# Swapping the operands of a one-hot product and pausing GpSimd's gathers of one more tile in a DLRM/CIN kernel

## The chip, the cores and the metric

The kernel runs on one NeuronCore of a Trainium2 chip. The time is device microseconds of one execution, the median of several runs; lower is better. TensorE (PE) multiplies matrices, with its weight loads counted apart as PEld; VectorE (DVE), ScalarE (ACT) and GpSimd (POOL) work on SBUF, and SyncE (SP), ACT and POOL issue DMAs.

## The reference, cut to what matters

A batch of 1,024 rows looks up 24 embedding tables of width 16. The embeddings go through a three-layer compressed interaction network (each layer multiplies the embeddings with the layer before, field by field, and mixes with weights), whose sums over the width go with a dense context through a small MLP.

```python
e = jnp.stack([tbl_0[ids[:, 0]], tbl_1[ids[:, 1]], ..., tbl_23[ids[:, 23]]], axis=1)   # (1024, 24, 16)
# _cin_forward(X0=e, Ws=(W0, W1, W2)), 64 outputs per layer
for W in Ws:
    H_prev = Xk.shape[1]
    Wr = W.reshape(F_, H_prev, W.shape[1])
    Xk = jnp.einsum('bfd,bhd,fho->bod', X0, Xk, Wr)
    outs.append(Xk.sum(axis=2))
z = jnp.concatenate(outs, axis=1)
h = jnp.concatenate([z, dense_ctx], axis=1)
h = jnp.maximum(h @ W_top1 + b_top1, 0.0)
h = jnp.maximum(h @ W_top2 + b_top2, 0.0)
y = h @ W_top3
```

Eight of the tables have 125,000 or 12,500 rows, sixteen have 1,000 or 1,250.

## The kernel before

All is float32. The batch is cut into 8 tiles of 128 rows, and each tile into two units of 64 rows, so there are 16 units. A tile's embeddings are brought into `x0_rows` (128 rows by 24 fields by 16), stored to DRAM in `x0_dram` (the profile's x_scratch), and loaded again from there in broadcast forms: `A` (three buffers of 128x1024 a unit) and `C` (two loads a unit, and a third buffer that ScalarE copies together, `copy_c`). VectorE multiplies A by C for the first layer (L373, three products a unit) and A by `ps_b`, a spread form of the first layer's output, for the second (L383, twelve a unit); each product Z is taken up by TensorE matmuls into `ps_x`. Z has a ring of five buffers. `ps_b` is made by TensorE (`make_b`) or, from unit 4 on, partly loaded (`B_sb`) and copied into PSUM by ScalarE.

**How tile 0 gets its embeddings.** Its eight large tables are gathered by GpSimd: one indirect DMA a table (L215), 8 in all, without a pause. Its sixteen small tables are looked up with one-hot matrices, in two sets of eight tables. A set's table rows are cut into chunks of 128 (8 chunks for set 0, 10 for set 1). For each chunk VectorE compares the ids with the chunk's row numbers (L346), which gives a 128x1024 matrix of ones and zeros in a buffer Z: 128 table rows by 8 tables by 128 batch rows. TensorE then runs 8 matmuls a chunk (L406, called at L612): the table chunk (128x16) is the operand that is loaded into the array, and the ones (128x128) stream. Results of the tables lie in four column groups of 32 of the array and accumulate in `ps_b[k]`. They come out turned (width by batch row), so ScalarE copies them to `x0_small` (L838, 4 copies a set), TensorE turns them (`turn_small`, L418, 2 transposes a set), and ScalarE copies the result to `x0_rows` (L842) and stores it (L206, on ACT's queue). 18 chunks of 8 matmuls are 144 matmuls; each float32 matmul shows as two LDWEIGHTS and two MATMUL records, so 288 pairs.

**What follows.** SP waits in order for the three parts of tile 0 and loads A and C of units 0 and 1. TensorE runs 40 transposes on the identity (`keep_warm`, L412) and the three first products; then the loop over units begins.

**How tiles 1 to 7 get theirs.** GpSimd gathers all 24 tables a tile, one indirect DMA each. Tile 1's gathers follow tile 0's at once. From tile 2 on, a gather is preceded by a pause: a memset of `pause_sb` (128x288, L227) and a wait for it. Tile 2's first also waits until tile 0 is stored. SP stores a tile when its 24 gathers have landed (`store_tile`, L206) and later waits for that store before it loads C and A of the tile's first unit. SP is in order: the loads of quarters, A, C and B of other units stand in the same queue.

```python
            for f in range(FR):
                gather(0, f, first_gathered)
            for t in range(1, TILES):
                if t >= 2:
                    wait_stored(pool, t - 2)
                for f in range(F):
                    if t >= 2:
                        pool.memset(pause_sb[:, :], 0.0).then_inc(paused, 1)
                        pool.wait_ge(paused, F * (t - 2) + f + 1)
```

Of the kernel before, what the change touches and what calls it, by code (L numbers as in the profile page):

```python
# [10 lines left out]
BATCH, F, D, H, DENSE = 1024, 24, 16, 64, 16  # L11
M1, M2 = 512, 256
TILE_ROWS = 128
# [11 lines left out]
FR, HR = 8, 16  # L25
# [7 lines left out]
ZR = 5  # L33
AS = 3
WARM = (40, 16, 16, 4)
SETS = 2
# [31 lines left out]
def cin_tower(nc, dense_t, ids, tables, small_ids, small_tables, small_rows, chunks, w0a, w0b, w1, w2, wt1, bt1, wt2, bt2, wt3, ident, mask, pick, out):  # L68

    CR = small_tables.shape[0]
# [5 lines left out]
    with ctx:  # L77
        def sb(name, shape, dt=F32):
            return ctx.enter_context(nc.sbuf_tensor(name, shape, dt))
# [4 lines left out]
        def sem(name):  # L84
            return ctx.enter_context(nc.semaphore(name))

        ids_sb = sb("ids_sb", [128, TILES * F], mybir.dt.int32)
        id_sb = sb("id_sb", [128, 128])
# [3 lines left out]
        small_sb = sb("small_sb", [CR, len(HOT), FR, D])  # L92
        small_rows_sb = sb("small_rows_sb", [CR, max(chunks)])
        small_ids_sb = [sb(f"small_ids_sb{k}", [CR, FR * TILE_ROWS], mybir.dt.int32) for k in range(SETS)]
        small_ids_f32 = [sb(f"small_ids_f32_{k}", [CR, FR * TILE_ROWS]) for k in range(SETS)]

        x0_small = [sb(f"x0_small{k}", [128, 2 * TILE_ROWS]) for k in range(SETS)]
        pause_sb = sb("pause_sb", [128, PAUSE])
        w0_sb = sb("w0_sb", [128, NI, H])
        w0m_sb = sb("w0m_sb", [128, NI, H])  # L100
# [10 lines left out]
        x0_rows = [sb(f"x0_rows{p}", [128, F * D]) for p in range(2)]  # L111
# [6 lines left out]
        Z = [sb(f"Z{r}", [128, COLS]) for r in range(ZR)]  # L118
# [16 lines left out]
        ps_b = [bank(f"ps_b{e}", 2) for e in range(2)]  # L135
        ps_x2, ps_x1, ps_tower = bank("ps_x2"), bank("ps_x1"), bank("ps_tower")

        ps_turn = bank("ps_turn")
# [10 lines left out]
        ident_in, mask_in, pick_in, w0_in, w1_in, tower_in = (sem(n) for n in (  # L149
            "ident_in", "mask_in", "pick_in", "w0_in", "w1_in", "tower_in"))  # L150
# [6 lines left out]
        paused = sem("paused")  # L157

        hot_used, small_turned = sem("hot_used"), sem("small_turned")  # L160
        z_used, b_made, x2_turned, x0_turned, g_summed = (sem(n) for n in (
            "z_used", "b_made", "x2_turned", "x0_turned", "g_summed"))
        z3_summed, h1_summed, h2_summed, y_summed = (sem(n) for n in (
            "z3_summed", "h1_summed", "h2_summed", "y_summed"))

        small_copied, small_ready = sem("small_copied"), sem("small_ready")
        c_copied, b_copied = sem("c_copied"), sem("b_copied")
        x1_copied, x2_copied, x2r_copied, diag_ready, g_copied = (sem(n) for n in (
            "x1_copied", "x2_copied", "x2r_copied", "diag_ready", "g_copied"))  # L170
# [4 lines left out]
        small_ids_ready, hot_ready = sem("small_ids_ready"), sem("hot_ready")  # L175
# [34 lines left out]
        @block.gpsimd  # L210
        def _(pool):
            pool.wait_ge(ids_in, 16)

            def gather(t, f, landed):
                pool.indirect_dma_start(  # L215
                    out=x0_rows[t % 2][:, f * D:(f + 1) * D], out_offset=None, in_=tables[f],
                    in_offset=bass.IndirectOffsetOnAxis(ap=ids_sb[:, t * F + f:t * F + f + 1], axis=0),
                ).then_inc(landed, 16)
# [4 lines that stand above are left out]
                if t >= 2:  # L223
                    wait_stored(pool, t - 2)
                for f in range(F):
                    if t >= 2:
                        pool.memset(pause_sb[:, :], 0.0).then_inc(paused, 1)  # L227
                        pool.wait_ge(paused, F * (t - 2) + f + 1)

                    after(pool, z_ready, PER_SLOT * (2 * t - 5) + 2 * PER_SLOT * f // F)  # L230
                    gather(t, f, gathered[t % 2])
# [102 lines left out]

        @block.vector
        def _(dve):
            for k in range(SETS):
                nc.vector.memset(x0_small[k][:, :], 0.0).then_inc(small_ids_ready, 1)
            dve.wait_ge(small_rows_in, 16)
            for n, (k, c) in enumerate(HOT):  # L340
                if c == 0:
                    dve.wait_ge(small_ids_in[k], 16)
                    nc.vector.tensor_copy(small_ids_f32[k][:, :], small_ids_sb[k][:, :]).then_inc(small_ids_ready, 1)
                    dve.wait_ge(small_ids_ready, SETS + k + 1)
                after(dve, hot_used, n - ZR + 1)
                nc.vector.tensor_scalar(Z[n % ZR][0:CR, :], small_ids_f32[k][:, :], small_rows_sb[:, c:c + 1],  # L346
                                        None, ALU.is_equal).then_inc(hot_ready, 1)
# [57 lines left out]
        def mm(out, lhsT, rhs, start=True, stop=True):  # L405
            return nc.tensor.matmul(out, lhsT, rhs, start=start, stop=stop)  # L406

        @block.tensor
        def _(pe):
            def keep_warm(n):  # L410
                for _ in range(n):
                    nc.tensor.transpose(ps_tower[:, 0:128], id_sb[:, :], id_sb[:, :])  # L412

            def turn_small(k):
                pe.wait_ge(ident_in, 16)
                pe.wait_ge(small_copied, 4 * (k + 1))
                for half in range(2):
                    last = nc.tensor.transpose((ps_turn, ps_x2)[k][:, TILE_ROWS * half:TILE_ROWS * (half + 1)],  # L418
                                               x0_small[k][:, TILE_ROWS * half:TILE_ROWS * (half + 1)], id_sb[:, :])
                last.then_inc(small_turned, 1)  # L420

            def cross1(u, i):
                s = made_x1(u, i) - 1
# [182 lines left out]
            for n, (k, c) in enumerate(HOT):  # L606
                if c == 0:
                    pe.wait_ge(small_in[k], 16)
                pe.wait_ge(hot_ready, n + 1)
                for f in range(FR):  # L610
                    g, half = f % 4, f // 4
                    last = mm(ps_b[k][32 * g:32 * g + D, 512 * half:512 * half + TILE_ROWS], small_sb[:, n, f, :],  # L612
                              Z[n % ZR][0:CR, TILE_ROWS * f:TILE_ROWS * (f + 1)], c == 0, c == chunks[k] - 1)
                last.then_inc(hot_used, 1)
                if c == 2 and k > 0:
                    turn_small(0)
            turn_small(SETS - 1)
            keep_warm(WARM[0])
            pe.wait_ge(w0_ready, 1)
            for i in range(NI):  # L620
# [28 lines left out]
        def _(act):  # L649
# [181 lines left out]
            act.wait_ge(mask_in, 16)  # L831

            nc.scalar.copy(first_sb[:, :], mask_sb[:, :])
            act.wait_ge(small_ids_ready, SETS)
            for k in range(SETS):
                act.wait_ge(hot_used, sum(chunks[:k + 1]))
                for g in range(4):
                    nc.scalar.copy(x0_small[k][32 * g:32 * g + D, :].rearrange("p (h b) -> p h b", h=2),  # L838
                                   ps_b[k][32 * g:32 * g + D, :].rearrange("p (h b) -> p h b", h=2)[:, :, 0:TILE_ROWS])\
                        .then_inc(small_copied, 1)  # L840
                act.wait_ge(small_turned, k + 1)
                nc.scalar.copy(x0_rows[0][:, FR * D * (k + 1):FR * D * (k + 2)].rearrange("p (f d) -> p f d", d=D),  # L842
                               (ps_turn, ps_x2)[k][:, 0:2 * TILE_ROWS].rearrange("p (f e) -> p f e", e=32)[:, :, 0:D])\
                    .then_inc(small_ready, 1)
                act.wait_ge(small_ready, k + 1)
                store_rows(act, 0, slice(FR * (k + 1), FR * (k + 2)), part_stored[k + 1])
# [90 lines left out]
```

## Time and profile before

| | |
|---|---|
| median of 3 runs | 413.58 us (409.85 to 417.03) |
| the profiled execution | 417.16 us, span from first to last instruction 415.3 us |
| mean granted TensorE clock | 0.992 of full speed |
| busy | PE 363.0 us (87%), DVE 302.4 (73%), ACT 184.6 (44%), POOL 231.3 (56%) |
| DMA | 71.07 MB, mean 171 GB/s |

The profile is one execution. Its page shows the span in 40 slices of 10.4 us; a timeline row gives start, duration, engine, line, operation, output and inputs, the count of merged instructions and, in brackets, the idle time before and what ended it. "issue" means that the engine waited for nothing that the profile shows. All times below are microseconds from the span's start. L12 is line 12 of the kernel before; behind the change the same code stands some lines higher.

### The profile page before, as it was taken

The numbers are of one execution on the slowest core, as the hardware profiler recorded it, in microseconds if no ns is written. First come the engines' busy times: TensorE is split into PE (matmuls) and PEld (weight loads), VectorE is DVE, ScalarE is ACT, GpSimd is POOL, SyncE is SP. The second block draws the span as 40 slices with busy tenths as digits, with TensorE's granted clock in tenths as the row PEclk, the third lists the DMA queues.
The fourth block names the chain that finished last, engine by engine and source line by source line (L and its number), as shares of the span: only waits on it lengthen the run. The fifth ranks groups of instructions, "written<-read, shape, count | busy, mean of one in ns | idle before, by whom it ended". The sixth has DMA issues, their size and how long they took to land.

```text
span 415.3 us, 6926 instructions
## 1 busy us (share of the span) xinstructions
PE 363.0 (87%) x2624; PEld 161.1 (39%) x2624; DVE 302.4 (73%) x299; ACT 184.6 (44%) x347; POOL 231.3 (56%) x324
## 2 busy tenths in 40 slices
PE   1531485999999999898999999999899999999997
PEld 0200372523323333344343434444343354443465
DVE  3210452599698989859798989989799999898700
ACT  1000110024362426444756566565457475745374
POOL 5777106888888888888878888888830000000000
PEclk9999998899999999999999999999999999999999
DMA  7520047969988798998799989997999899941000
GB/s 217 154 42 6 2 96 170 243 134 230 209 214 208 178 242 153 235 243 196 155 227 244 240 162 228 257 253 145 234 252 261 156 238 239 225 117 36 2 1 4
DMA packets 56884, 71.07 MB, mean 171 GB/s; under 512 B 31153, under 2 KB 36017, under 8 KB 56850
## 3 DMA queue, kind: packets, MB, share of 16 engines
q1 hardware_dynamic: 49138, 69.04, 71.7%
q0 software_dynamic: 5632, 1.45, 3.4%
q8 instruction: 21, 0.34, 0.4%
q10 hardware_dynamic: 2080, 0.13, 0.3%
q14 instruction: 13, 0.11, 0.1%
HBM read 50.15 MB, written 1.58 MB: 125 GB/s over the span
## 4 chain that ended last, share of the span: by engine, by line
PE 80%; issue 9%; DMA 4%; ACT 3%; DVE 2%; another core or an unknown queue 2%; SPq 0%; DVEq 0%; ACTq 0%
PE ps_x L406 48%; PE ps_b L406 12%; PE ps_tower L406 9%; PE ps_turn L406 6%; PE ps_turn L459 2%; DMA x_scratch<-x_rows 1%; PE ps_turn L467 1%; DMA small_ids_sb<-small_ids 1%; DVE Z L383 1%; DMA C<-x_scratch 1%; PE ps_tower L412 1%; DVE Z L373 1%; ACT x_diag L691 1%; ACT C L665 0%
## 5 line engine op out<-in xcount | busy, mean ns | idle before, releaser
L383 DVE TENSOR_TENSOR Z<-A,ps_b 128x1024 f32<-128x1024 f32 x192 | 221.8, 1213 | 18.9 <-PE ps_x L406 13.6
L215 POOL DMA_INDIRECT x_rows<-tbl,ids_sb x176 | 180.4, 1025 | 52.7 <-issue 23.9
L406 PE MATMUL ps_x<-Z,w_sb 128*64 128x512 f32 x768 | 184.9, 598 | 0.9 <-DVE Z L383 0.5
L406 PEld LDWEIGHTS ps_x<-Z,w_sb 128*64 128x64 f32 x768 | 49.4, 136 | 80.8 <-issue 58.9
L373 DVE TENSOR_TENSOR Z<-A,C 128x1024 f32<-128x1024 f32 x48 | 57.4, 1222 | 30.5 <-DMA C<-x_scratch 10.4
L227 POOL MEMSET pause_sb<- 128x288 f32 x144 | 50.7, 352 | 21.4 <-DMA x_scratch<-x_rows 21.3
L691 ACT ACTIVATE x_diag<-ps_turn,mask_sb 128x192 f32<-128x192 f32 x128 | 50.6, 605 | 12.2 <-PE ps_turn L467 11.6
L406 PE MATMUL ps_b<-Z,small_sb 128*16 128x128 f32 x288 | 21.1, 357 | 34.7 <-issue 25.2
L406 PE MATMUL ps_x<-Z,w0s_sb 128*64 128x512 f32 x192 | 46.3, 608 | 5.5 <-DVE Z L373 5.3
L704 ACT COPY G<-ps_turn 128x416 f32<-128x416 f32 x31 | 15.7, 506 | 61.4 <-PE ps_turn L406 42.8
L674 ACT COPY ps_b<-B_sb 128x1024 f32<-128x1024 f32 x36 | 37.1, 1030 | 0.0
L346 DVE TENSOR_SCALAR Z<-small_ids_f,small_rows_sb 128x1024 f32<-128x1024 f32 x18 | 12.7, 750 | 33.3 <-remote 31.5
L406 PEld LDWEIGHTS ps_turn<-x_diag,x_rows 128*64 128x64 f32 x496 | 24.8, 137 | 20.6 <-issue 19.5
L406 PE MATMUL ps_b<-x_sb,pick_sb 64*128 64x512 f32 x112 | 31.3, 639 | 0.2 <-issue 0.2
L655 ACT COPY x_sb<-ps_x 128x512 f32<-128x512 f32 x16 | 9.4, 587 | 47.4 <-PE ps_x L406 47.4
L406 PE MATMUL ps_turn<-x_diag,x_rows 128*64 128x104 f32 x496 | 27.8, 254 | 1.7 <-issue 1.6
L406 PEld LDWEIGHTS ps_b<-Z,small_sb 128*16 128x16 f32 x288 | 12.3, 119 | 42.9 <-issue 32.1
L406 PEld LDWEIGHTS ps_x<-Z,w0s_sb 128*64 128x64 f32 x192 | 13.5, 139 | 33.3 <-issue 23.2
L838 ACT COPY x_small<-ps_b 16x256 f32<-16x256 f32 x8 | 2.9, 364 | 49.3 <-PE ps_b L406 49.1
L664 ACT COPY C<-C 64x1024 f32<-64x1024 f32 x15 | 15.6, 1043 | 7.6 <-DMA C<-x_scratch 7.3
L406 PE MATMUL ps_tower<-h,wt_sb 128*64 128x256 f32 (+1 forms) x112 | 15.5, 379 | 0.4 <-ACT h L774 0.4
L665 ACT COPY C<-C 64x1024 f32<-64x1024 f32 x15 | 15.7, 1044 | 0.4
(60 smaller groups left out, 192.7 us busy)
## 6 DMA issues: line engine op xcount, KB each, us to landing
A<-x_scratch SPq DMA_DIRECT2D x48, 512.0 KB
B_sb<-x_sb SPq DMA_DIRECT2D x72, 256.0 KB
C<-x_scratch SPq DMA_DIRECT2D x32, 512.0 KB
x_rows<-tbl,ids_sb POOLq DMA_INDIRECT x176
x_quarters<-x_scratch SPq DMA_DIRECT2D x16, 96.0 KB
x_scratch<-x_rows SPq DMA_DIRECT2D x7, 192.0 KB
small_ids_sb<-small_ids SPq DMA_DIRECT2D x2, 512.0 KB, 5.2
w_sb<-w SPq DMA_DIRECT2D x2, 384.0 KB
```

What stands on the lines that cost most here:

```text
L215: pool.indirect_dma_start(out=x0_rows[t % 2][:, f * D:(f + 1) * D], out_offset=None, in_=tables[f], in_offset=bass.IndirectOffsetOnAxis(ap ...
L227: pool.memset(pause_sb[:, :], 0.0).then_inc(paused, 1)
L346: nc.vector.tensor_scalar(Z[n % ZR][0:CR, :], small_ids_f32[k][:, :], small_rows_sb[:, c:c + 1], None, ALU.is_equal).then_inc(hot_ready, 1)
L373: nc.vector.tensor_tensor(Z[s % ZR][:, :], A[u % AS][i][:, :], C[u % 2][i][:, :], ALU.mult).then_inc(z_ready, 1)
L383: nc.vector.tensor_tensor(Z[s % ZR][:, :], A[u % AS][i][:, :], ps_b[j % 2][:, :], ALU.mult)\
L406: return nc.tensor.matmul(out, lhsT, rhs, start=start, stop=stop)
L655: nc.scalar.copy(x1_sb[u % 2][:, :], ps_x1[:, :]).then_inc(x1_copied, 1)
L664: nc.scalar.copy(c[NI - 1][0:64, :], c[1][64:128, :]).then_inc(c_copied, 1)
L665: nc.scalar.copy(c[NI - 1][64:128, :], c[0][0:64, :]).then_inc(c_copied, 1)
L674: nc.scalar.copy(ps_b[(k + 1) % 2][:, :], B_sb[k][:, :]).then_inc(b_copied, 1)
L691: last = nc.scalar.activation(x0_diag[u % 2][:, :, 0:F, b].rearrange("p (h k) f -> p k h f", k=2), ps_turn[:, 0:256].rearrange("p (k f h) ...
L704: nc.scalar.copy(G[:, :, at:at + ROWS_Q].rearrange("p j (k b) -> p k j b", b=RB), bank[:, 0:KB * J3 * RB].rearrange("p (k j b) -> p k j b" ...
```

## The change

Three things. (1) In tile 0's one-hot matmuls the operands trade places: the ones (128x128) are loaded into the array and the table chunk (128x16) streams. The result comes out as batch row by width, eight tables side by side in 128 columns of `ps_b[k]`, and one accumulation group runs over all of a set's matmuls. (2) What turned the result goes: the two memsets of `x0_small`, 4 copies a set, `turn_small`, and their semaphores; one ScalarE copy a set brings `ps_b[k]` to `x0_rows`. (3) The pause stands ahead of each gather of tile 1 too.

```diff
@@ gpsimd
                 for f in range(F):
-                    if t >= 2:
-                        pool.memset(pause_sb[:, :], 0.0).then_inc(paused, 1)
-                        pool.wait_ge(paused, F * (t - 2) + f + 1)
+                    pool.memset(pause_sb[:, :], 0.0).then_inc(paused, 1)
+                    pool.wait_ge(paused, F * (t - 1) + f + 1)
 
                     after(pool, z_ready, PER_SLOT * (2 * t - 5) + 2 * PER_SLOT * f // F)
                     gather(t, f, gathered[t % 2])
@@ vector
-            for k in range(SETS):
-                nc.vector.memset(x0_small[k][:, :], 0.0).then_inc(small_ids_ready, 1)
             dve.wait_ge(small_rows_in, 16)
@@ tensor
-            def turn_small(k):
-                pe.wait_ge(ident_in, 16)
-                pe.wait_ge(small_copied, 4 * (k + 1))
-                for half in range(2):
-                    last = nc.tensor.transpose((ps_turn, ps_x2)[k][:, TILE_ROWS * half:TILE_ROWS * (half + 1)],
-                                               x0_small[k][:, TILE_ROWS * half:TILE_ROWS * (half + 1)], id_sb[:, :])
-                last.then_inc(small_turned, 1)
...
                 for f in range(FR):
-                    g, half = f % 4, f // 4
-                    last = mm(ps_b[k][32 * g:32 * g + D, 512 * half:512 * half + TILE_ROWS], small_sb[:, n, f, :],
-                              Z[n % ZR][0:CR, TILE_ROWS * f:TILE_ROWS * (f + 1)], c == 0, c == chunks[k] - 1)
+
+                    last = mm(ps_b[k][:, D * f:D * (f + 1)], Z[n % ZR][0:CR, TILE_ROWS * f:TILE_ROWS * (f + 1)],
+                              small_sb[:, n, f, :], (c, f) == (0, 0), (c, f) == (chunks[k] - 1, FR - 1))
                 last.then_inc(hot_used, 1)
-                if c == 2 and k > 0:
-                    turn_small(0)
-            turn_small(SETS - 1)
+            pe.wait_ge(ident_in, 16)
             keep_warm(WARM[0])
@@ scalar
-            act.wait_ge(small_ids_ready, SETS)
             for k in range(SETS):
                 act.wait_ge(hot_used, sum(chunks[:k + 1]))
-                for g in range(4):
-                    nc.scalar.copy(x0_small[k][32 * g:32 * g + D, :].rearrange("p (h b) -> p h b", h=2),
-                                   ps_b[k][32 * g:32 * g + D, :].rearrange("p (h b) -> p h b", h=2)[:, :, 0:TILE_ROWS])\
-                        .then_inc(small_copied, 1)
-                act.wait_ge(small_turned, k + 1)
-                nc.scalar.copy(x0_rows[0][:, FR * D * (k + 1):FR * D * (k + 2)].rearrange("p (f d) -> p f d", d=D),
-                               (ps_turn, ps_x2)[k][:, 0:2 * TILE_ROWS].rearrange("p (f e) -> p f e", e=32)[:, :, 0:D])\
+                nc.scalar.copy(x0_rows[0][:, FR * D * (k + 1):FR * D * (k + 2)], ps_b[k][:, 0:FR * D])\
                     .then_inc(small_ready, 1)
```

GpSimd's order at the start, before. L215 is a gather, L227 the pause; x_rows is `x0_rows`.

```order
L215 DMA x_rows<-tbl,ids_sb 128x16 x32
L227 MEMSET pause_sb 128x288
L215 DMA x_rows<-tbl,ids_sb 128x16
L227 MEMSET pause_sb 128x288
L215 DMA x_rows<-tbl,ids_sb 128x16
```

GpSimd's order at the start, with the change (the gather is L213, the pause L224):

```order
L213 DMA x_rows<-tbl,ids_sb 128x16 x8
L224 MEMSET pause_sb 128x288
L213 DMA x_rows<-tbl,ids_sb 128x16
L224 MEMSET pause_sb 128x288
L213 DMA x_rows<-tbl,ids_sb 128x16
```

The run of gathers without a pause shrinks from 32 to 8; 24 pauses come in.

TensorE's order from its first matmul to the first product, before; the shape behind a matmul is rows of the result by columns streamed:

```order
L406 MATMUL ps_b<-Z,small_sb 16x128 x88
L418 MATMUL ps_turn<-id_sb,x_small 128x128 x2
L406 MATMUL ps_b<-Z,small_sb 16x128 x56
L418 MATMUL ps_x<-id_sb,x_small 128x128 x2
L412 MATMUL ps_tower<-id_sb 128x128 x40
L406 MATMUL ps_x<-Z,w0s_sb 64x512 x2
```

TensorE's order in the same place, with the change:

```order
L401 MATMUL ps_b<-small_sb,Z 128x16 x144
L407 MATMUL ps_tower<-id_sb 128x128 x40
L401 MATMUL ps_x<-Z,w0s_sb 64x512 x2
```

The 144 matmuls stand in one run, and the four transposes are gone. Nothing behind them moved.

ScalarE's order from the first copy of a result of tile 0 to its second store, before:

```order
L838 COPY x_small<-ps_b 16x256 x4
L842 COPY x_rows<-ps_turn 128x128
L206 DMA x_scratch<-x_rows 128x8x16
L838 COPY x_small<-ps_b 16x256 x4
L842 COPY x_rows<-ps_x 128x128
L206 DMA x_scratch<-x_rows 128x8x16
```

ScalarE's order in the same place, with the change:

```order
L821 COPY x_rows<-ps_b 128x128
L204 DMA x_scratch<-x_rows 128x8x16
L821 COPY x_rows<-ps_b 128x128
L204 DMA x_scratch<-x_rows 128x8x16
```

One copy a set stands where five copies and a wait for TensorE stood.

## Rows read from the trace of the kernel before

**Rows 1.** The page, slices of 10.4 us: PE and DMA, busy share in tenths
```profile
PE   1531485999999999898999999999899999999997
...
DMA  7520047969988798998799989997999899941000
```

**Rows 2.** The page's groups: one-hot matmuls and VectorE's comparisons (busy, mean ns, idle before)
```profile
L406 PE MATMUL ps_b<-Z,small_sb 128*16 128x128 f32 x288 | 21.1, 357 | 34.7 <-issue 25.2 <-DVE Z L346 9.3
...
L346 DVE TENSOR_SCALAR Z<-small_ids_f,small_rows_sb 128x1024 f32<-128x1024 f32 x18 | 12.7, 750 | 33.3 <-remote 31.5
```

**Rows 3.** Timeline of PE, 8 to 60 us
```profile
9.28 4.05 PE L406 MATMUL ps_b<-Z,small_sb 128*16 128x128 f32 x59 [9.28 <-DVE Z L346]
14.15 0.62 PE L406 MATMUL ps_b<-Z,small_sb 128*16 128x128 f32 x4 [0.82 <-issue]
...
44.56 0.37 PE L406 MATMUL ps_b<-Z,small_sb 128*16 128x128 f32 x1 [1.73 <-issue]
...
48.06 4.50 PE L406 MATMUL ps_b<-Z,small_sb 128*16 128x128 f32 x80 [1.03 <-issue]
...
52.87 3.25 PE L406 MATMUL ps_b<-Z,small_sb 128*16 128x128 f32 x112
```

**Rows 4.** Timeline of GpSimd: first and last gathers of tiles 0 to 2, and tile 7's last
```profile
3.01 1.08 POOL L215 DMA_INDIRECT x_rows<-tbl,ids_sb  x1 [2.56 <-DMA ids_sb<-ids]
...
12.25 1.02 POOL L215 DMA_INDIRECT x_rows<-tbl,ids_sb  x1 [0.31 <-issue]
...
42.53 0.94 POOL L215 DMA_INDIRECT x_rows<-tbl,ids_sb  x1 [0.30 <-issue]
...
64.79 0.34 POOL L227 MEMSET pause_sb<- 128x288 f32 x1 [21.31 <-DMA x_scratch<-x_rows]
...
65.47 0.95 POOL L215 DMA_INDIRECT x_rows<-tbl,ids_sb  x1 [0.34 <-POOL pause_sb L227]
...
67.04 0.95 POOL L215 DMA_INDIRECT x_rows<-tbl,ids_sb  x1 [0.27 <-POOL pause_sb L227]
...
103.61 0.95 POOL L215 DMA_INDIRECT x_rows<-tbl,ids_sb  x1 [0.27 <-POOL pause_sb L227]
...
304.75 0.95 POOL L215 DMA_INDIRECT x_rows<-tbl,ids_sb  x1 [0.27 <-issue]
```

**Rows 5.** Timeline of PE: short matmuls elsewhere, all at full clock
```profile
58.11 4.53 PE L412 MATMUL ps_tower<-id_sb 128*128 128x128 f32 x40
...
191.86 0.88 PE L406 MATMUL ps_turn<-x_diag,x_rows 128*64 128x104 f32 x16
...
387.68 0.88 PE L406 MATMUL ps_turn<-x_diag,x_rows 128*64 128x104 f32 x16
```

**Rows 6.** Timeline, all engines: from the last one-hot matmul to unit 0's first product
```profile
56.19 1.53 ACT L838 COPY x_small<-ps_b 16x256 f32<-16x256 f32 x4 [2.94 <-PE ps_b L406]
...
58.31 0.27 ACT L842 COPY x_rows<-ps_x 128x128 f32<-128x128 f32 x1 [0.59 <-PE ps_x L418]
58.60 0.37 ACTq L206 DMA_DIRECT2D x_scratch<-x_rows  x1
...
79.29 6.88 DVE L383 TENSOR_TENSOR Z<-A,ps_b 128x1024 f32<-128x1024 f32 x6 [0.59 <-PE ps_b L406]
```

**Rows 7.** SP's waits: total us, times, longest us
```profile
SPq L206 <- DMA x_rows<-tbl,ids_sb: 20.0, 2, 14.6
```

**Rows 8.** The chain of waits: one load of C from issue to landing
```profile
64.66 4.56 DMA C<-x_scratch
```

**Rows 9.** Timeline of SP and ScalarE: stores of tiles 2 and 7, unit 14's C
```profile
112.18 0.36 SPq L206 DMA_DIRECT2D x_scratch<-x_rows  x1
...
315.97 0.76 SPq L206 DMA_DIRECT2D x_scratch<-x_rows  x1
...
325.02 1.18 SPq L263 DMA_DIRECT2D C<-x_scratch  x2
...
333.99 1.04 ACT L664 COPY C<-C 64x1024 f32<-64x1024 f32 x1
```

More of the change, by code:

```diff
@@ L95, in cin_tower @@
         small_ids_f32 = [sb(f"small_ids_f32_{k}", [CR, FR * TILE_ROWS]) for k in range(SETS)]
-        x0_small = [sb(f"x0_small{k}", [128, 2 * TILE_ROWS]) for k in range(SETS)]
         pause_sb = sb("pause_sb", [128, PAUSE])
@@ L157, in cin_tower @@
         paused = sem("paused")
-        hot_used, small_turned = sem("hot_used"), sem("small_turned")
+        hot_used = sem("hot_used")
         z_used, b_made, x2_turned, x0_turned, g_summed = (sem(n) for n in (
@@ L164, in cin_tower @@
             "z3_summed", "h1_summed", "h2_summed", "y_summed"))
-        small_copied, small_ready = sem("small_copied"), sem("small_ready")
+        small_ready = sem("small_ready")
         c_copied, b_copied = sem("c_copied"), sem("b_copied")
@@ L343, in _ @@
                     nc.vector.tensor_copy(small_ids_f32[k][:, :], small_ids_sb[k][:, :]).then_inc(small_ids_ready, 1)
-                    dve.wait_ge(small_ids_ready, SETS + k + 1)
+                    dve.wait_ge(small_ids_ready, k + 1)
                 after(dve, hot_used, n - ZR + 1)
```

## Prediction, made before the result was known

> **What bounds the kernel now.** I read the page's slices first, then its groups, then the timeline of the first 80 us engine by engine, and last SP's waits. In the slices [rows 1] PE is busy in eight or nine tenths from the ninth slice on (83 us) to nearly the end, and DMA as well from the seventh; in the third to fifth slice (21 to 52 us) neither is. The start is what is slow: the first product of unit 0 begins at 79.29 [rows 6], a fifth of the span. The groups name the place [rows 2]: the one-hot matmuls have 25.2 us of "issue" idle before them, and VectorE waits 31.5 us before its comparisons, though 18 of them at 0.75 us need 12.7 us.
>
> The timeline of PE [rows 3] shows how: 59 records in 4.05 us, then ever fewer, 4 with a gap of 0.82 us behind at 14.15, single ones with 1.7 us of gap at 44.56, and at 48.06 all at once 80 in 4.50 us (VectorE's pace) and 112 in 3.25 us. 288 - 80 - 112 = 96 records took until 48. The last 37 of them took 34 us, and they are the same instructions as the fast ones. What changed at 48.06 is on GpSimd [rows 4]: the run of 32 gathers without a pause began at 3.01 and its last was issued at 42.53. Tile 1's 24 came every (42.53 - 12.25) / 24 = 1.26 us. If something behind a gather needs a fixed time and PE's instructions wait for the same thing, that time is (48.06 - 3.01) / 32 = 1.41 us, a backlog grows by 0.15 us a gather, and its end lies 4.6 us behind the end of the last gather, as it does. I call it the stall and do not know its resource. Paused gathers come every 67.04 - 65.47 = 1.57 us, longer than 1.41, so they should build no backlog; and 144 of them (64.79 to 305.70) run beside matmuls that are not slowed: 16 short records take 0.88 us at 191.86 among gathers and 0.88 us at 387.68 without any [rows 5].
>
> **The change part by part.** The sum is made against the profiled execution, 417.16 us (span 415.3 plus 1.9), which lies 3.6 above the median of 413.58.
>
> *Pauses, on PE.* The stall goes, except what the first 8 gathers leave: 3.01 + 8 x 1.41 = 14.3, while the ninth gather would now be issued at about 12.25 + 1.02 + 0.35 + 0.27 = 13.9. That backlog of 0.4 us shrinks by 0.16 a gather and is gone near 18.5. At four records in 0.62 + 0.82 us [rows 3] from 13.3 to 18.5 PE would lose some 4 us; with a smaller backlog I take 2.5, bounds 0 and 4.
>
> *Operands swapped.* A pair now loads 128 columns and streams 16, and all 8 tables use the whole width, where before they lay in four column groups (112 records in 3.25 us, 29 ns each, less than 128 columns of one stream could take at the pace of [rows 5]). No row shows a 128-column load with 16 streamed. The nearest is the 40 transposes, 128 loaded and 128 streamed: 4.53 / 40 = 113 ns, 0.44 ns a column [rows 5]. By columns, 144 make 64 ns. 288 x 64 ns = 18.3 us. Upper end: a short stream costs as much as a long one, 288 x 113 ns = 32.5 us. Lower end: VectorE's pace, 18 x 0.75 + 0.8 for a cast + the last chunk's 1.0, 15.3 us less the 0.9 that it starts ahead, 14.4. I take 18.3: the columns explain both shapes that I can see. The last one-hot matmul then ends at 9.28 + 18.3 + 2.5 = 30.1, against 56.1 (52.87 + 3.25): 26.0 us earlier.
>
> *Fewer steps behind it.* From 56.1 to the store at 58.60 there were four copies (1.53 us), two transposes and a copy [rows 6], 2.5 us. Now there is one copy of 0.27 us and some 0.1 of hand-over: 2.1 less. Set 0's chain shrinks alike and isn't last. The two memsets on VectorE lie ahead of the ids' arrival and cost nothing either way.
>
> So the second store goes out near 30.5, 28 us earlier. From there to unit 0's first product were 79.29 - 58.60 = 20.7 us of store, loads, three products and two spreads; I leave them, so that product comes at about 51.
>
> *Pauses, on GpSimd.* Queued behind each new wait are all later gathers, and behind them SP's stores of tiles 1 to 7. Tile 1's end moves from 43.5 to 13.3 + 24 x 1.57 = 51.0, and to 52 with some contention against VectorE's comparisons (gathers took 1.02 to 1.08 us beside them and 0.94 later [rows 4]). Its store was not waited for before, and with SP reaching it near 45 it is now late by some 8 us, but it stood behind a queue of loads anyway. Tile 2's gathers no longer wait for the store of tile 0 (21.31 us idle at 64.79) and start at 52: **12.8 us earlier, not 28.** From then on GpSimd is the slow one. It ran from 64.79 to 305.70 without a stop, 240.9 / 144 = 1.67 us a gather, 40 us a tile, and two units take PE the same 40 us. So the gathers move by 12.8 and the units may move by that plus the slack between them. SP waited for gathers in tiles 2 and 3 [rows 7]: tile 2's last ended at 104.56 and the store went out at 112.18 [rows 4, 9], 7.6 us of landing. For tile 7 that gives 305.70 + 7.6 = 313.3 against a store at 315.97: 2.7 of slack. Its C was issued at 325.02 and copied at 333.99; one load lands in 4.56 [rows 8], two need between that and 9.0, so the slack there is 0 to 4.4, I take 2.3. Another 1 lies in Z's ring ahead of PE. Together 6, bounds 3 and 10.
>
> *Sum:* 12.8 + 6 = 18.8 us off, less than the 28 that the start gives. 417.2 - 18.8 = 398.4 for an execution like the profiled one; on the median 413.6 - 18.8 = **395**.
>
> **The rivals.**
>
> *Gathers don't bind* (28 us reach the end): while SP waits, the queues of loads drain, so landing takes less than 7.6 us and slack is found at each tile. For it: no VectorE wait in tiles 2 and 3 names a load although SP waited 20 us there. Against: the 15 us of difference would have to be found within 40-us tiles in which both engines are full. Time: 413.6 - 28 = 385.5.
>
> *The pair costs 113 ns:* the run ends at 9.28 + 32.5 + 2.5 = 44.3, 11.8 earlier, with the tail 13.9; that is about what gathers allow. Time: 400.
>
> *The stall stays, and is longer* (slower): if what holds PE is any run of gathers on an idle machine and not their pace, it lasts as long as they do, now until 52 + 4.6 = 56.6 instead of 48. Some 188 pairs at 64 ns are then left, 12.0 us: the run ends at 68.6 instead of 56.1, 12.5 later, and with the tail 10.4. Time: 424. It decides from the point where fewer than about 60 more pairs get through before 56. For it: all paused gathers in the trace run beside a PE whose instructions are long. Against: the short ones in [rows 5]. A milder form, PE at the early pace of 4 records in 1.44 us to 55, ends the run near 62, with the tail 4 later: within 2%.
>
> **How the numbers follow.** Forecast 0.50; gathers don't bind 0.20; pair at 113 ns 0.10; mild stall 0.08; full stall 0.12. A measurement here tells about 2% (8.3 us) from no change, since runs before spread from 409.85 to 417.03. Faster by over 2%: 0.80; within 2%: 0.08; slower: 0.12. The range takes in the free case (385.5, and slack of 10 gives 391) and the dear pair (400, with weaker slack 404) and reaches towards the mild stall: 384 to 410, leaving out the full stall and most of the mild one.
>
> **What would show it right or wrong.** In the profile after: one-hot records without growing gaps after 14 us and a last one near 30; pairs at 64 ns (78 or 113 would correct that term); ScalarE's second store near 30.5; unit 0's first L383-type product near 51; tile 1's last gather ending near 52 and tile 7's near 293; SP waiting for gathers in most tiles, well over 20 us in total. Wrong: PE's gaps still there until past 50 (the stall is not a matter of pace), tile 7's gathers at 293 with the end still 28 us earlier (slack was larger), or VectorE held in the first units by tile 1's late store.

## The result, and the profile after

| | before | after |
|---|---|---|
| median | 413.05 us of 4 runs (409.85 to 417.03) | 423.01 us of 4 runs (421.09 to 424.51) |
| the profiled execution | 417.16 us, span 415.3 | 421.09 us, span 419.0 |
| ratio after / before | | 1.027, 95% interval 1.019 to 1.035 |

The change makes the kernel slower by some 10 us, clear of no change; that it is over 2% is likely, and the interval does not settle it. I had forecast 395 us, with 384 to 410 as the range and faster by over 2% as the likeliest verdict. On another chip the comparison gave 1.028 (1.017 to 1.039), below. A profile shows one execution, which can lie in the slower of two states: those of the pause alone (404.79 us) and of the short pause on the third chip (424.87) are 7 to 8 us above their medians.

First the slices of the page of after, beside [rows 1]:

```profile
PE   1999999889999999989999999999899998999997
PEld 1999999622322333444343433544443453443466
...
DMA  7522300997999799899899989998999899941000
```

PE no longer idles at 21 to 52 us, as it did in [rows 1]: it is full from the second slice. But so is PEld, the load of the array, for six slices, and nowhere else in the program. DMA starts a slice later than before. PE is busy for 398.8 us in after against 363.0, and not because it has more to do. The groups name the instructions (busy us, mean ns of one, idle before):

```profile
L401 PE MATMUL ps_b<-small_sb,Z 128*128 128x16 f32 x288 | 61.6, 374 | 9.3 <-DVE Z L341 9.3
L401 PEld LDWEIGHTS ps_b<-small_sb,Z 128*128 128x128 f32 x288 | 61.5, 333 | 9.3 <-DMA small_sb<-small_tables 9.3
```

In [rows 2] the same 288 were busy for 21.1 us, with 25.2 us of "issue" idle before them. That idle time is gone whole. The timeline of PE shows the price:

```profile
9.31 61.59 PE L401 MATMUL ps_b<-small_sb,Z 128*128 128x16 f32 x288 [9.31 <-DVE Z L341]
70.74 5.83 PE L407 MATMUL ps_tower<-id_sb 128*128 128x128 f32 x40
```

One row without a gap: 61.59 / 288 = **214 ns a pair**, from the first to the last. The kernel before needed 25 such rows, with gaps up to 2.4 us, of which [rows 3] shows some. Behind it the 40 transposes take 5.83 us, where [rows 5] had 4.53; we come back to that. What waited for this run, in the timeline of ScalarE and VectorE:

```profile
70.94 0.27 ACT L821 COPY x_rows<-ps_b 128x128 f32<-128x128 f32 x1 [33.87 <-PE ps_b L401]
71.24 0.37 ACTq L204 DMA_DIRECT2D x_scratch<-x_rows  x1
...
87.09 5.75 DVE L378 TENSOR_TENSOR Z<-A,ps_b 128x1024 f32<-128x1024 f32 x5 [0.59 <-PE ps_b L401]
```

The second store goes out at 71.24 instead of 58.60 [rows 6], 12.6 us later, and unit 0's first product starts at 87.09 instead of 79.29, 7.8 later. The chain of waits shows where most of the difference of 4.8 us between the two was won back (start, duration, what):

```profile
9.31 61.60 PE ps_b L401 x288
71.24 2.15 DMA x_scratch<-x_rows
73.41 4.58 DMA C<-x_scratch
```

In before the chain has `58.60 6.04 DMA x_scratch<-x_rows` at this place. At 71 us no DMA is busy (slice seven reads 0), so the store lands 3.9 us sooner. Last, GpSimd: tile 1's last gather, and tile 2's first pause.

```profile
53.70 1.05 POOL L213 DMA_INDIRECT x_rows<-tbl,ids_sb  x1 [0.27 <-POOL pause_sb L224]
73.53 0.34 POOL L224 MEMSET pause_sb<- 128x288 f32 x1 [18.78 <-DMA x_scratch<-x_rows]
...
313.76 0.95 POOL L213 DMA_INDIRECT x_rows<-tbl,ids_sb  x1 [0.27 <-POOL pause_sb L224]
```

Tile 1's gathers end at 54.8 (53.70 + 1.05), but tile 2's wait for the late store of tile 0 and start 8.7 us later than in [rows 4]; tile 7's last is issued 9.0 us later. The profiled executions themselves differ by 3.9 us, the medians by 10.

### The profile page after: what moved, and what is told of

Same layout as the page of the kernel before. It is cut to its first block, busy times and chain, and to the rows that moved or that the text cites. A ratio compares the mean times of both kernels' runs of the same rounds, so it can differ in the third digit from the quotient of the medians.

```text
span 419.0 us, 6929 instructions
## 1 busy us (share of the span) xinstructions
PE 398.8 (95%) x2620; PEld 208.5 (50%) x2620; DVE 305.2 (73%) x297; ACT 181.9 (43%) x339; POOL 243.6 (58%) x348
## 3 DMA queue, kind: packets, MB, share of 16 engines
q0 software_dynamic: 5632, 1.45, 3.1%
## 4 chain that ended last, share of the span: by engine, by line
PE 79%; DMA 6%; DVE 4%; ACT 4%; issue 3%; another core or an unknown queue 2%; SPq 1%; DVEq 0%; ACTq 0%
PE ps_x L401 41%; PE ps_b L401 22%; PE ps_tower L401 8%; PE ps_turn L401 6%; DMA B_sb<-x_sb 3%; DVE Z L378 2%; PE ps_turn L446 2%; DVE Z L368 2%; PE ps_turn L454 1%; DMA small_ids_sb<-small_ids 1%; DMA C<-x_scratch 1%; ACT ps_b L659 1%; ACT x_diag L676 1%; DMA x_scratch<-x_rows 1%
## 5 line engine op out<-in xcount | busy, mean ns | idle before, releaser
L213 POOL DMA_INDIRECT x_rows<-tbl,ids_sb x176 | 180.7, 1027 | 51.9 <-POOL pause_sb L224 30.4
L224 POOL MEMSET pause_sb<- 128x288 f32 x168 | 62.7, 373 | 18.9 <-DMA x_scratch<-x_rows 18.8
L401 PE MATMUL ps_b<-small_sb,Z 128*128 128x16 f32 x288 | 61.6, 374 | 9.3 <-DVE Z L341 9.3
L401 PEld LDWEIGHTS ps_b<-small_sb,Z 128*128 128x128 f32 x288 | 61.5, 333 | 9.3 <-DMA small_sb<-small_tables 9.3
L401 PE MATMUL ps_x<-Z,w0s_sb 128*64 128x512 f32 x192 | 45.2, 597 | 2.2 <-DVE Z L368 2.0
L341 DVE TENSOR_SCALAR Z<-small_ids_f,small_rows_sb 128x1024 f32<-128x1024 f32 x18 | 16.1, 913 | 29.3 <-PE ps_b L401 29.3
```

What stands on the lines that cost most here:

```text
L213: pool.indirect_dma_start(out=x0_rows[t % 2][:, f * D:(f + 1) * D], out_offset=None, in_=tables[f], in_offset=bass.IndirectOffsetOnAxis(ap ...
```

## The experiments

The kernels ran in three groups, each on a chip of its own, with the kernel before in the same group: 413.86 us on the first chip, 388.55 on the second, 413.69 on the third. The second of these numbers was not expected and is treated below.

**The pause alone, and the swap alone.** The first is before with this edit, the second is after without it.

```
-                    if t >= 2:
-                        pool.memset(pause_sb[:, :], 0.0).then_inc(paused, 1)
-                        pool.wait_ge(paused, F * (t - 2) + f + 1)
+                    pool.memset(pause_sb[:, :], 0.0).then_inc(paused, 1)
+                    pool.wait_ge(paused, F * (t - 1) + f + 1)
```

> The kernel before with the pause ahead of tile 1's gathers, operands as before. Theory A (the stall is a matter of the gathers' pace, 1.26 us against 1.57): the one-hot matmuls end near 27 instead of 56 us, the second store goes out near 29, then gathers bind and the median is 392 to 398 us. Theory B (the stall comes with any run of gathers while nothing else runs): it lasts as long as the gathers, to 54 + 4, and the median is 420 or more. Theory C (only a few us change): 409 to 415.

Measured: 397.52 us (396.38 to 404.79), ratio 0.961 (0.956 to 0.966). PE's timeline, in which no gap of "issue" is left behind the third row (three rows are cut):

```profile
9.45 4.07 PE L405 MATMUL ps_b<-Z,small_sb 128*16 128x128 f32 x58 [9.45 <-DVE Z L345]
14.34 0.63 PE L405 MATMUL ps_b<-Z,small_sb 128*16 128x128 f32 x4 [0.83 <-issue]
15.79 6.77 PE L405 MATMUL ps_b<-Z,small_sb 128*16 128x128 f32 x114 [0.81 <-issue]
...
27.31 0.63 PE L405 MATMUL ps_b<-Z,small_sb 128*16 128x128 f32 x16 [0.44 <-DVE Z L345]
```

Two gaps of 0.8 us remain, in place of the many of [rows 3], and the run ends at 27.9 instead of 56.1. Unit 0's first product starts at 48.48, 30.8 us earlier, and yet the end comes only 16 earlier. SP's waits say why, beside [rows 7]:

```profile
SPq L206 <- DMA x_rows<-tbl,ids_sb: 51.4, 5, 15.3
```

SP waits for gathers five times instead of twice, 51.4 us in total instead of 20.0. Both halves of this part of the prediction hold: the pause removes the stall, and behind it the gathers bind.

> The changed kernel without the pause ahead of tile 1's gathers. If each pair costs 213 ns whatever GpSimd does (load of 128 float32 columns), the one-hot matmuls again end near 71 us and the median is that of the changed kernel, 421 to 425. If part of the 213 ns is the stall in another form, pairs are dearer while gathers run, to 48 us, and the run ends later: over 428. If the pauses themselves cost something, it is faster than the changed kernel by their delay, 1 to 3 us.

Measured: 442.41 us (439.45 to 448.24), ratio 1.069 (1.059 to 1.079). PE's timeline:

```profile
9.23 18.71 PE L402 MATMUL ps_b<-small_sb,Z 128*128 128x16 f32 x87 [9.23 <-DVE Z L342]
...
41.82 0.19 PE L402 MATMUL ps_b<-small_sb,Z 128*128 128x16 f32 x1 [2.62 <-issue]
...
48.17 39.87 PE L402 MATMUL ps_b<-small_sb,Z 128*128 128x16 f32 x187 [0.51 <-issue]
```

The stall is there again, and lets go at 48.17 as in [rows 3]. A stalling PE now has pairs of 215 and 213 ns on both sides of it. So the four kernels make a table (the corner with both edits was measured on its own chip, by ratios): pause alone 0.961, swap alone 1.069, both 1.027. The pause is worth 16 us on its own and some 17 with the swap; the swap costs 27 to 29 us either way. In the medians the two edits add up. At the end of the one-hot run they don't: 56.1 before, 27.9 with the pause alone, 88.0 with the swap alone, and 70.9 with both. The pause moves that end by 28 us without the swap and by 17 with it, and without the swap the gathers then hold back 12 of the 28. So that the sum comes out is in part luck.

**Why a pair takes 214 ns.** Three kernels change the shape of the pair. The first loads 64 columns twice instead of 128 once, into two halves of the array:

```
-                    last = mm(ps_b[k][:, D * f:D * (f + 1)], Z[n % ZR][0:CR, TILE_ROWS * f:TILE_ROWS * (f + 1)],
-                              small_sb[:, n, f, :], (c, f) == (0, 0), (c, f) == (chunks[k] - 1, FR - 1))
+                    for e in range(2):
+                        at = TILE_ROWS * f + 64 * e
+                        last = mm(ps_b[k][64 * e:64 * (e + 1), D * f:D * (f + 1)], Z[n % ZR][0:CR, at:at + 64],
+                                  small_sb[:, n, f, :], (c, f) == (0, 0), (c, f) == (chunks[k] - 1, FR - 1))
```

> The changed kernel with each load of 128 ones-columns split in two of 64, into the two halves of the array, so twice as many matmuls. Theory A (213 ns is four array cycles a loaded column at 2.4 GHz, and halves load side by side or faster): 32 to 54 ns a record, 576 records in 18 to 31 us, the last near 28 to 42 us, median 393 to 402. Theory B (a load costs by columns, halves one after the other): 107 ns a record, the run ends at 71 again, 421 to 425. Theory C (213 ns is a fixed cost of a pair of this kind): 123 us, median near 475.

Measured: 401.38 us (398.45 to 403.79), ratio 0.973 (0.966 to 0.980). PE's timeline:

```profile
17.33 25.31 PE L401 MATMUL ps_b<-small_sb,Z 128*64 128x16 f32 x457 [0.26 <-issue]
...
45.00 6.91 PE L407 MATMUL ps_tower<-id_sb 128*128 128x128 f32 x40
```

55 ns a record, 111 for the two that stand for one pair: half of 214, for the same columns loaded and twice as many streamed. So the number of columns loaded doesn't give the price by itself, unless two loads into different halves run side by side; that they do is my reading, and no run shows it apart. The transposes behind, at 6.91 us, are slow once more.

The second keeps the full load and streams 128 columns instead of 16. It also puts other numbers into tile 0's embeddings, since each product now takes all eight tables.

```
-                    last = mm(ps_b[k][:, D * f:D * (f + 1)], Z[n % ZR][0:CR, TILE_ROWS * f:TILE_ROWS * (f + 1)],
-                              small_sb[:, n, f, :], (c, f) == (0, 0), (c, f) == (chunks[k] - 1, FR - 1))
+                    last = mm(ps_b[k][:, 0:FR * D], Z[n % ZR][0:CR, TILE_ROWS * f:TILE_ROWS * (f + 1)],
+                              small_sb[:, n, :, :].rearrange("p f d -> p (f d)"), (c, f) == (0, 0),
+                              (c, f) == (chunks[k] - 1, FR - 1))
```

> The changed kernel with all 8 tables' chunks (128 columns) streamed past each block of ones instead of the one table's 16; every product is summed into the same 128 columns, so tile 0's small-table embeddings are other numbers. It tells the load from the stream in the 213 ns. If the load alone makes them and hides the stream, a pair stays at 213 ns. If load and stream follow each other at two cycles a column, 112 more columns add 93 ns: 306. At one cycle a column: 260. If 213 ns were load 107 + a fixed minimum of 107 for any stream, it stays at 213 too.

Measured: 398.96 us in one run. PE's timeline, and its windows (stretch, length, then busy us and count of PE and of PEld, VectorE, ScalarE, GpSimd, granted clock, DMA share, GB/s):

```profile
9.27 34.66 PE L401 MATMUL ps_b<-small_sb,Z 128*128 128x128 f32 x288 [9.27 <-DVE Z L341]
43.77 4.53 PE L407 MATMUL ps_tower<-id_sb 128*128 128x128 f32 x40
```
```profile
9.00:13.00 4.00, 3.73 (x17) 3.76 (x18) 2.78 (x5) 0.00 (x0) 3.08 (x4) 1.00 1.01 356
13.00:20.00 7.00, 7.00 (x61) 7.00 (x60) 3.88 (x5) 0.00 (x0) 5.92 (x9) 1.00 0.39 88
```

Eight times the streamed columns, and the run ends at 43.9 instead of 70.9. The first 17 pairs take 219 ns, as in after; the next 61 take 7.00 / 61 = 115. In after no pair ever gets there. Behind those wide streams the same pair goes almost twice as fast (a single load falls from 333 ns to 192), and the transposes that follow are at [rows 5]'s 4.53 us.

**Is it the clock?** The granted clock of the after profile reads 1.00 in every window from 10 to 70 us, which seemed to exclude it. So the third kernel, on the second chip, puts 40 transposes between the first and the second set of after:

```
+                if n == chunks[0] - 1:
+                    pe.wait_ge(ident_in, 16)
+                    keep_warm(40)
```

> The changed kernel with 40 transposes of the identity on TensorE between set 0's and set 1's one-hot matmuls. Theory H (a run of 16-column streams leaves the array at its low clock, 1.2 GHz, where a pair costs 213 ns; at 2.4 GHz it costs 107): the transposes begin at some 213 ns each and end at 113, the first pairs of set 1 cost 107 ns, and after a while the cost goes back to 213. Theory F (213 ns is the fixed price of such a pair): the transposes change nothing, set 1's 160 pairs take 34.2 us as before, and the run ends about 6 us later than in the changed kernel.

Measured: 429.84 us in one run. Its windows behind the transposes (36.54 to 42.5), columns as above:

```profile
44.00:46.00 2.00, 2.00 (x20) 2.00 (x19) 0.90 (x1) 0.00 (x0) 1.73 (x4) 1.00 0.79 162
46.00:48.00 2.00, 2.00 (x12) 2.00 (x13) 0.83 (x1) 0.00 (x0) 1.73 (x3) 0.57 0.07 13
48.00:50.00 2.00, 2.00 (x11) 2.00 (x11) 0.76 (x1) 0.00 (x0) 1.73 (x3) 0.50 0.07 6
50.00:60.00 10.00, 10.00 (x49) 10.00 (x48) 3.99 (x23) 0.00 (x0) 4.08 (x6) 0.50 0.04 3
```

Here the record does show it. Right behind the transposes the pairs take 2.00 / 20 = 100 ns at a granted clock of 1.00 (2.4 GHz). Then, with PE busy without a gap but on 16-column streams, the granted clock falls to 0.50 (1.2 GHz), and the same pairs take 10.00 / 49 = 204 ns by the records of this window, 22.90 / 109 = 210 by those from 50 us to the end of the run. That is close to the pace of after from its first pair, 214. Single loads say the same (name, count, then ns least/median/most, first and last start), first those at a shown 1.00, then those at 0.50:

```profile
L401 PEld LDWEIGHTS ps_b<-small_sb,Z x28: 191/192/193, 42.9 to 45.9; 128*128 128x128 f32 x28
```
```profile
L401 PEld LDWEIGHTS ps_b<-small_sb,Z x48: 333/334/334, 49.9 to 59.9; 128*128 128x128 f32 x48
```

The group of after had 333 as the mean of all 288. It follows that after's run is at 1.2 GHz although its column reads 1.00. The transposes behind it agree: their matmuls take 421 ns up to 72.7 us and 272 from 73 on. The record seems not to show the state in which the program starts. The kernel before gives a second case: from 48.6 to 51.9 us its products take 417 to 421 ns each at a shown 1.00 on one chip, and the same at a shown 0.50 in its profile on the third chip:

```profile
48.00:52.00 4.00, 3.95 (x74) 3.67 (x76) 3.75 (x6) 1.46 (x4) 0.00 (x0) 0.50 0.00 0
```

The last of this kind is after with four transposes behind each chunk's products, from the second chunk on:

```
+                if n == 1:
+                    pe.wait_ge(ident_in, 16)
+                if n >= 1:
+                    keep_warm(4)
```

> The changed kernel with 4 transposes of the identity after each chunk's 8 one-hot matmuls, from the second chunk on. Theory H: once the clock is up a chunk takes 16 x 0.107 + 4 x 0.11 = 2.2 us instead of 3.4; if 4 transposes a chunk are enough to hold it up, the last one-hot matmul ends near 50 us instead of 71 and the time is about 405 us or less; if they are not enough, every chunk costs 3.4 + 0.9 and the run ends near 87. Theory F: 3.4 + 0.5 a chunk, near 79.

Measured: 430.98 us in one run. Every chunk looks like the first:

```profile
17.09 3.43 PE L401 MATMUL ps_b<-small_sb,Z 128*128 128x16 f32 x16
20.36 1.09 PE L407 MATMUL ps_tower<-id_sb 128*128 128x128 f32 x4
```

214 ns a pair throughout, and the last product ends at 82.9 us. Four wide transposes among 16 narrow pairs did not raise the clock here, and only added their own time.

**How slow must gathers be?** Two kernels pause less: every fourth gather of tile 1 alone, and every gather with half the memset.

```
-                    if t >= 2:
+                    if t >= 2 or f % 4 == 3:
...
-                        pool.wait_ge(paused, F * (t - 2) + f + 1)
+                        pool.wait_ge(paused, F * (t - 2) + f + 1 + F // 4 if t >= 2 else f // 4 + 1)
```

> The kernel before with the pause ahead of every fourth gather of tile 1 only, so that its gathers come every 1.34 us on average. If each gather occupies what TensorE waits for by 1.41 us, a backlog still grows, by 0.07 us a gather, and TensorE is free again at 3.0 + 32 x 1.41 = 48 us as in the kernel before, though the last gather ends near 45.5; in between it gets more done than before, since the backlog is half as long. If instead any pause breaks the stall, TensorE runs freely after each one and its one-hot matmuls end before 35 us.

Measured: 389.49 us in one run, on the second chip. It told nothing on the pace, because the kernel before takes 388.55 us there (386.53 to 391.62, 13 runs), 25 less than on the other chips. No profile of the kernel before was taken on that chip, so that its 25 us are the stall is inferred. The profile of the every-fourth kernel, with tile 1's gathers 1.42 us apart on average and three of four unpaused, has no stall: `9.30 7.90 PE L406 MATMUL` holds 176 records without a gap. The second kernel is the pause alone with this edit too:

```
-PAUSE = 288
+PAUSE = 144
```

> The kernel with only the pause of tile 1 added (397.5 us), with the pause of all tiles cut from 288 to 144 columns. A paused gather should come every 1.45 to 1.48 us instead of 1.57, still more than 1.41, so no stall, and the 168 gathers end 15 to 20 us earlier. If gathers bind the kernel, it is 5 to 12 us faster than 397.5, the rest being bound by TensorE: 386 to 392. If they don't, 397. If 1.47 is too close to 1.41, TensorE stalls in the start and it is over 400.

Measured on the second chip: 385.98 us (383.35 to 389.42), ratio 0.992 (0.989 to 0.996). So I repeated what matters on a third chip: before, after, the pause alone, and the short pause.

> The kernel before, unchanged, for its profile on this chip. The job before this one ran on another chip, and there the kernel before took 388.6 us instead of 413. Theory S (whether TensorE stalls beside unpaused gathers is a property of the chip): where it takes 413, its one-hot matmuls end at 56 us as in the first profile; where it takes 389, they end near 23 us with no growing gaps, and everything else is alike.

> The changed kernel, unchanged, with rounds. Its own start has no stall on either kind of chip, so it should take 421 to 425 us on both. Beside a kernel before of 413 that is 2.5% slower, beside one of 389 it is 8 to 9% slower.

> The kernel before with the pause ahead of tile 1's gathers and nothing else. On a chip with the stall 397 us (4% faster, as measured). On a chip without it the pause buys nothing and delays the gathers by some 8 us, which bind: 392 to 398 against 389, 1 to 2% slower.

> As the last, with all pauses cut to 144 columns (a gather every 1.45 us). On a chip without the stall 386 us, as measured. On a chip with it: if 1.45 us is slower than the 1.41 at which its backlog stays away, 386 to 392; if not, over 400.

Measured: before 413.64 us in its profiled run, where the stall is as in [rows 3] to the microsecond:

```profile
42.44 0.37 PE L406 MATMUL ps_b<-Z,small_sb 128*16 128x128 f32 x1 [2.40 <-issue]
...
48.05 4.46 PE L406 MATMUL ps_b<-Z,small_sb 128*16 128x128 f32 x76 [0.31 <-issue]
```

After 427.75 us (421.6 to 428.0), ratio 1.028 (1.017 to 1.039); the pause alone 396.29 us (394.6 to 400.17), ratio 0.958 (0.952 to 0.964); the short pause 417.09 us (412.11 to 424.87), ratio 1.004 (0.999 to 1.009). With the short pause tile 1's gathers come every 1.45 us at best and every 1.55 on average, and PE's timeline has this:

```profile
23.29 11.55 PE L405 MATMUL ps_b<-Z,small_sb 128*16 128x128 f32 x77 [0.81 <-issue]
```
```profile
20.00:30.00 10.00, 7.65 (x54) 1.78 (x49) 2.26 (x3) 0.00 (x0) 8.34 (x13) 0.50 0.31 60
```

The stall is milder than in before but costs more than the gaps that the timeline shows: 77 records take 150 ns each. The granted clock is 0.50 there, but that is not the reason, since at 0.50 the kernel before on this chip gets 76 records through in 4.46 us, 59 ns each, and VectorE is busy for only 2.26 of the 10 us. So PE is held inside a row that reads as busy. The run ends near 47. A pause of half the length gives back nothing on this chip, and it is in all tiles, where further gaps come (4.5 us of "issue" at 101 us).

## Why the prediction was wrong, point by point

*The stall, and that it goes with the pause* was right. The 1.41 us were fitted to the release at 48.06; that the swap alone has it at 48.17 and before on another chip at 48.05 repeats the same order of gathers and does not test them. But PE's own rows in the trace of before show such a beat:

```profile
29.10 0.37 PE L406 MATMUL ps_b<-Z,small_sb 128*16 128x128 f32 x1 [1.05 <-issue]
30.53 0.37 PE L406 MATMUL ps_b<-Z,small_sb 128*16 128x128 f32 x1 [1.05 <-issue]
31.94 0.37 PE L406 MATMUL ps_b<-Z,small_sb 128*16 128x128 f32 x1 [1.04 <-issue]
33.33 0.37 PE L406 MATMUL ps_b<-Z,small_sb 128*16 128x128 f32 x1 [1.02 <-issue]
```

From 26.98 to 48.06 single products start one to four steps of 0.70 us apart, 30 steps in 21.08 us. Twice the step is 1.41, while gathers start every 1.25 us there. With the pause the stall is gone but for 1.6 us of gaps (2.0 on the third chip), where I had taken 2.5. As a threshold 1.41 fails: with the short pause no gather of tile 1 follows the one before it by less than 1.45 us, by my sum no backlog grows, and PE is held until near 47. The pace that is enough lies above that one (1.55 us on average) and at or below that of the pause alone, whose gathers in tile 1 are 1.57 us apart at the least and 1.75 on average, on the chips that stall.

*The pair of the swap* is the step that failed: "by columns, 144 make 64 ns", with an upper end of 113 ns. It measured 214. Two things are in it. At 2.4 GHz the pair takes 100 ns (the window from 44 to 46 us), against 113 for the transposes with 112 more columns streamed, so the stream adds next to nothing and nearly all of the price goes with the full-width load; I had read 0.44 ns a column off the transposes as load plus stream, when the two overlap. With that the run would take some 30 us. The other factor of two is the clock, which had no term in my sum at all: the program starts at 1.2 GHz, in before too, and in after it stays there through all 288 pairs. The upper end, "a short stream costs as much as a long one", came from rows "all at full clock", as I named the group myself, for a stretch at the program's start. The trace of before had the warning, one view deeper than I went: its one-hot matmuls taken singly, at 9 to 13 us, at 49 to 52 and at 53 to 56.

```profile
L406 PE MATMUL ps_b<-Z,small_sb x59: 369/421/421, 9.3 to 12.9; 128*16 128x128 f32 x59
```
```profile
L406 PE MATMUL ps_b<-Z,small_sb x64: 417/421/421, 48.6 to 51.9; 128*16 128x128 f32 x64
```
```profile
L406 PE MATMUL ps_b<-Z,small_sb x112: 272/273/283, 52.9 to 55.9; 128*16 128x128 f32 x112
```

Up to 52 us the one-hot products of before run at the low clock too, where one record takes up to 421 ns instead of 272. There it cost little, since PE waited for VectorE or stood in the stall.

By the sum: the run takes 61.6 us instead of 18.3 + 2.5, and ends at 70.9 instead of 30.1.

*The Trainium skill's rules* that I weighed, page TensorE: Matmul & The Clock Gate, gave me 78 ns a pair and 22.5 us, too small as well. The 53 ns for a load were my own halving: the Trainium skill's section "LDWEIGHTS (loading the stationary operand)", on the same page, gives columns divided by 1.2, which for 128 is an estimated 107 ns, and names no clock for it. A pair here, load and stream together, measured 100 ns at 2.4 GHz and 214 at 1.2, in these float32 products. The remark of the Trainium skill on small results in distinct column groups (the same page, "Packing small matmuls") is what the trace bears out best: 29 ns a pair in four groups at 2.4 GHz; at 1.2 GHz it is 111 for two halves and 214 for the full width.

*Fewer steps behind it:* the hand-over from the last product to the store measured 0.3 us (70.9 to 71.24) against 2.5, as I had it.

*From the store to unit 0* I kept 20.7 us. It was 87.09 - 71.24 = 15.9, for the most part since the store landed in 2.15 us, on idle DMAs, instead of 6.04. The tail of the loss was softened by that, from 12.6 to 7.8.

*The gathers bind:* right, where the start is early enough. The pause alone is this forecast without the swap, and it measured 397.5 and 396.3 us for my 395. That is 16.3 and 17.4 us off for my 18.8, which is near, though not every term is right. The run there ends at 27.9 and not at 30.1, and tile 2's first gather starts at 55.90 instead of 65.47, so 9.6 us earlier and not 12.8 (10.0 on the third chip); the rest, for which I had 6 us of slack, is then some 7. Tile 1's last gather of after was issued at 53.70 and ended at 54.8; I had its end at 52. The pauses cost more than planned beside VectorE's comparisons, 0.79 us instead of 0.35, eight times in tile 1 of after. In after this path doesn't bind the start: tile 2's gathers wait 18.78 us for the store of tile 0.

*The rivals.* The measured 423.0 us is near the 424 of "the stall stays, and is longer", and that rival is still false: no gap of "issue" is left in the run. The time agrees only because the late end (70.9, there 68.6) came by another way. "The pair costs 113 ns" was the rival with the right place and the wrong size. None of mine had the clock in it.

The trace and the runs leave open what PE and the gathers share, why one chip of three is free of it, and what in a full-width load makes its price. I tried no kernel for that.

## What to carry to other kernels

Holding the big operand and streaming the small one turns a matmul into a load: before such a swap, price the load at the full width and at the low clock. Here 61.6 us of 16-column streams ran at 1.2 GHz from the first to the last, though the engine read as full. Take the price of an instruction from a stretch in the same clock state as the place where it will stand; at the start of these programs that was the low one even where the clock's column reads 1.00. And test two edits apart: here one was worth 16 us, the other cost 27, and on the two chips that stall the best kernel of the study is before with the pause alone, at 0.958 to 0.961 of its time. On the chip without the stall it was not run.

## What the runs showed of the hardware that was not expected

- The granted clock can read 1.00 from the start of the program while durations are those of 1.2 GHz: in after 333 ns a load, which in another of the runs is 192 at a shown 1.00 and 334 at a shown 0.50.
- A busy PE did not keep its clock: with no gap, but 16 columns a stream, it fell from 1.00 to 0.50 behind the transposes, and in after it never rose in 61.6 us of a full PE.
- Matmuls stall beside back-to-back gathers on some chips and, as far as the runs show, not on another. The kernel with the short pause has the stall in its profile on the third chip and not on the second. The same kernel before takes 388.6 us on one and 413.7 to 413.9 on two others; the one with the short pause takes 386.0 and 417.1.
- In the stall single products of PE start in steps of 0.70 us, half of 1.41, while the gathers start every 1.25 us.
- GpSimd's memset takes 0.79 us instead of 0.35 where one of VectorE's comparisons or casts lies beside it (the one at 16.80 us beside the comparison from 16.33 to 17.32), while most gathers stay at 0.95. VectorE pays too: that comparison takes 0.99 us, where those without a memset beside them take 0.75.
